# An attention and feed-forward layer in float32: the product with Wf in three F32R terms, and a new order of the steps around it

## What is computed

```python
Q = split_heads(x, 16); K = split_heads(x @ Wk + bk, 16); V = split_heads(x @ Wv + bv, 16)   # V: 1024 wide
o = softmax(Q @ K.T + causal_mask) @ V                       # per head, merged to 1024 features
x = layernorm(x + (x + gelu(o) @ Wf + bf))                   # exact gelu, Wf: 1024 x 256
h = silu(x @ wg.T / 127) * (x @ wu.T / 127)                  # 768 hidden features, integer weights
out = layernorm(x + h @ wd.T / 127)
```

## Time and profile before

| | us |
|---|---|
| runs (three) | 1847.09, 1849.84, 1851.43; median 1849.84 |
| the profiled execution | 1849.75 |
| its span (first to last instruction) | 1848.0 |
| TensorE busy | 1762.1 (95%) |
| VectorE busy | 1396.5 (76%) |
| GpSimd busy | 1221.8 (66%) |
| ScalarE busy | 1050.4 (57%) |

### The profile page before, as it was taken

How to read it: one execution, slowest core, us unless ns; L and a number is a source line. 1 busy time by engine, 2 the same in 40 slices (tenths; PEclk the granted TensorE clock), 3 DMA queues, 4 the chain that set the end, 5 groups by cost and what they waited for, 6 DMA issues and landing times. The chain is left out here.

```text
span 1848.0 us, 37611 instructions
## 1 busy us (share of the span) xinstructions
PE 1762.1 (95%) x10304; PEld 961.4 (52%) x10304; DVE 1396.5 (76%) x3417; ACT 1050.4 (57%) x1375; POOL 1221.8 (66%) x1146
## 2 busy tenths in 40 slices
PE   7999999999999999999999999888889999999996
PEld 5444444444444444444444444333466767676763
DVE  4787877778787787777778787886467878787864
ACT  2465665665565565665666565555545555555552
POOL 3488888888888888888888888999512222222221
PEclk9999999999999999999999999999999999999998
DMA  9675657556565655646556565563477565756500
GB/s 323 160 232 160 181 141 203 161 161 188 142 176 170 168 160 159 195 139 185 169 148 196 145 174 143 144 183 99 138 201 175 172 170 172 169 172 170 171 24 23
DMA packets 261152, 303.16 MB, mean 164 GB/s; under 512 B 28240, under 2 KB 177872, under 8 KB 261072
## 3 DMA queue, kind: packets, MB, share of 16 engines
q1 hardware_dynamic: 261072, 302.19, 58.3%
HBM read 174.20 MB, written 127.93 MB: 163 GB/s over the span
## 5 line engine op out<-in xcount | busy, mean ns | idle before, releaser
L802 POOL TENSOR_TENSOR weight_sum<-weight_sum,weights 128x512 f32<-128x512 f32 (+1 forms) x444 | 731.9, 1649 | 151.9 <-DVE weight_sum L1347 115.3
L1161 ACT ACTIVATE weights<-ring 128x1024 f32<-128x1024 f32 x576 | 570.7, 1026 | 221.2 <-PE ring L846 217.8
L846 PE MATMUL o_acc<-weights,v_pair 128*64 128x512 f32 (+3 forms) x3072 | 586.3, 501 | 17.1 <-POOL weights L757 16.4
L837 POOL TENSOR_TENSOR h_lo<-hidden,h_hi 128x512 f16<-128x512 f32 x96 | 114.4, 1193 | 390.2 <-ACT h_hi L1099 390.2
L1312 DVE TENSOR_REDUCE part_max<-ring 128x2 f32<-128x1024 f32 x256 | 301.0, 1217 | 86.4 <-PE ring L846 86.4
L846 PEld LDWEIGHTS o_acc<-weights,v_pair 128*64 128x64 f32 x3072 | 188.3, 136 | 302.7 <-issue 257.0
L1321 DVE CUSTOM_DVE_ANT_0 scrap<-ring,causal,part_max 128x256 bf16<-128x256 f32 (+3 forms) x512 | 251.3, 547 | 70.7 <-PE ring L846 70.4
L1321 DVE CUSTOM_DVE_ANT_0 scrap<-ring,causal 128x128 bf16<-128x128 f32 (+3 forms) x512 | 225.1, 486 | 91.1 <-PE ring L846 90.6
L846 PE MATMUL ring<-q_stack,k_stack 50*128 50x512 f32 (+3 forms) x1536 | 264.3, 382 | 26.1 <-DVE part_max L1312 17.6
L846 PE MATMUL ring<-k_stack,q_stack 48*128 48x512 f32 (+3 forms) x1536 | 256.9, 373 | 0.1
L846 PE MATMUL ring<-wf_sb,g 128*128 128x256 f32 x1024 | 230.5, 380 | 2.6 <-DVE y_pre L1416 1.7
(11 more groups left out here) (125 smaller groups left out, 2070.1 us busy)
## 6 DMA issues: line engine op xcount, KB each, us to landing
v_pairs<-v_unit SPq DMA_DIRECT2D x64, 512.0 KB, 3.5
v_pair<-v_pairs SPq DMA_DIRECT2D x64, 512.0 KB, 5.1
o_heads<-o_pair SPq DMA_DIRECT2D x64, 512.0 KB, 3.2
g<-o_heads SPq DMA_DIRECT2D x16, 2048.0 KB, 8.1
den_wide<-reciprocals SPq DMA_DIRECT2D x32, 1024.0 KB, 13.3
q_stack<-q_rows SPq DMA_DIRECT2D x128, 192.0 KB, 3.7
k_stack<-k_rows SPq DMA_DIRECT2D x128, 192.0 KB, 4.4
q_rows<-x_hi SPq DMA_DIRECT2D x28, 512.0 KB, 3.6
```

Of the source, the lines that this page charges most:

```text
L802: pool.tensor_tensor(dst, other, weights(t), ALU.add).then_inc(s_add, 1)
L837: pool.tensor_tensor(h_lo[:, f], h32[f % 2][:], h_hi[:, f], ALU.subtract).then_inc(s_hl, 1)
L846: return nc.tensor.matmul(o, l, r, start=start, stop=stop)
L1161: nc.scalar.activation(W[i][:], bank_of("t", i)[:], ACT.Exp).then_inc(s_w, 1)
```

## The change

Wf is split once into `wf_hi` and `wf_lo` (VectorE, in the drain of attention). Gelu's result is rounded by VectorE into `dn` (the buffer of the reciprocals, which are used by then) and the rest is made by GpSimd into `g`. TensorE multiplies with Wf as the stationary side and 512 tokens moving, 3 x 8 products for each half of the 256 features; the result has features on the partitions. x is loaded transposed, the residual sum `y_preT` is made in that layout, TensorE transposes it back, ScalarE copies it out. In the order: the products of unit r+1 now stand first on VectorE, ahead of z_pre; all Gelus are first on ScalarE; z of unit r-1 is made one step later; Wf's two halves stand around the transposes of y, and the transposes back between gate and up blocks 2 and 3; down goes over its six blocks for tiles 0 and 2 (two banks) and then 1 and 3. The stage has one step more (`STEPS_C = UNITS + 2`). The core of the diff:

```diff
 SyncE
 def load_g(r, it):                       # for unit r, issued two steps ahead
-    sp.wait_ge(s_wf, UT * (n - 1)); sp.wait_ge(s_y, UT * (n - 1))
+    sp.wait_ge(s_wf, DC * (n - 1)); sp.wait_ge(s_y, DC * (n - 1))
-    sp.dma_start(xn[r % 2][:], x[bass.ds(n * U, U), :].rearrange("(i p) d -> p i d", p=P))
+    sp.dma_start(xn[r % 2][:], xT[bass.ds(b, 1), :, t0:t0 + U].rearrange("o (c p) t -> (o p) c t", p=P))
 def load_dn(r, it):
-    sp.wait_ge(s_gn, HC * (n - 1))
+    sp.wait_ge(s_wf, DC * (n - 1))
 def finish(r, it):
-    if r >= 1: wait z of unit n - 1, store it
+    if r >= 2: wait z of unit n - 2, store it
 GpSimd
+def g_low(r, n, pairs):
+    for i in pairs:
+        pool.wait_ge(s_ghi, HC // 2 * n + i + 1)
+        pool.tensor_tensor(g[r % 2][:, 2*i:2*i+2], g_in[r % 2][:, 2*i:2*i+2],
+                           dn[r % 2][:, 2*i:2*i+2].bitcast(F32), ALU.subtract).then_inc(s_glo, 1)
 def attend(r, it):
+    if r == PAIRS + LEAD: g_low(0, 0, range(HC // 2))       # behind the last sums
 def finish(r, it):
+    if r + 1 < UNITS: g_low(r + 1, n + 1, range(0, HC // 2 - 1))
     ...                                                     # six h_lo of unit n - 1
+    if r + 1 < UNITS: g_low(r + 1, n + 1, range(HC // 2 - 1, HC // 2))
 TensorE
-def wf_product(r, n, tiles): ...
+def wf_product(r, n, d):
+    if d == 0 and r > 0: pe.wait_ge(s_yp, 2 * n)
+    for c in range(HC):
+        if d == 0 and c % 2 == 0: pe.wait_ge(s_ghi, HC // 2 * n + c // 2 + 1)
+        for k, w in enumerate((wf_hi, wf_lo)):
+            mm(rg[0][:, d], w[:, c, cols], dn[r % 2][:, c], c + k == 0, False)
+    for c in range(HC):
+        if d == 0 and c % 2 == 0: pe.wait_ge(s_glo, HC // 2 * n + c // 2 + 1)
+        e = mm(rg[0][:, d], wf_hi[:, c, cols], g[r % 2][:, c], False, c == HC - 1)
+    e.then_inc(s_wf, 1)
+def transpose_back(r, n):
+    pe.wait_ge(s_y, DC * (n + 1))
+    ...                                                     # 8 transposes of y_preT into ring0
 def attend(r, it):
-    if r == PAIRS + LEAD and b in (1, 3, 4): wf_product(0, 0, (max(b - 1, 1),))
+    if r == PAIRS + LEAD and b in (4, 5): wf_product(0, 0, b - 4)
 def down(m):
-    for i in range(UT):
-        for f in range(FC): ...
+    for tiles in ((0, 2), (1, 3)):
+        for f in range(FC): ...
 def finish(r, it):
-    wf_product(r, n, (0, 1)); transpose_y(r - 1, n - 1); wf_product(r, n, (2,))
-    gate_up(r - 1, n - 1); wf_product(r, n, (3,)); down(n - 1)
+    wf_product(r, n, 0); transpose_y(r - 1, n - 1); wf_product(r, n, 1)
+    gate_up(r - 1, n - 1, range(0, FC // 2)); transpose_back(r, n)
+    gate_up(r - 1, n - 1, range(FC // 2, FC)); down(n - 1)
 ScalarE
 def finish(r, it):
+    def copy_back():                                        # waits for s_yb; two copies of 128x512 into y_pre
+    if r + 1 < UNITS: gelus(r + 1, n + 1)
     ...                                                     # y_hi, Silu and h_hi as before
+    if f == 2 and r < UNITS: copy_back()
-    if r + 1 < UNITS: gelus(r + 1, n + 1)
     ...                                                     # logarithm and exponential
 VectorE
+def split_wf():
+    v.tensor_copy(wf_hi[:], wf_in[:])
+    v.tensor_tensor(wf_lo[:], wf_in[:], wf_hi[:].bitcast(F32), ALU.subtract)
+def g_high(r, n, pairs):
+    for i in pairs:
+        dve.wait_ge(s_gelu, HC * n + 2 * i + 2)
+        v.tensor_copy(dn[r % 2][:, 2*i:2*i+2], g_in[r % 2][:, 2*i:2*i+2]).then_inc(s_ghi, 1)
 def attend(r, it):
+    if r == PAIRS + LEAD and b == 0: g_high(0, 0, range(HC // 2))
+    if b == 0 and r == PAIRS + 1: split_wf()
 def finish(r, it):                                          # the new order
+    if r == 0: add_x()
+    norm(r + 1, it, range(HC // 2))
+    ...                                                     # waits for down, 4 x z_pre of unit n - 2
+    norm(r + 1, it, range(HC // 2, HC))
+    g_high(r + 1, n + 1, range(0, HC // 4))
+    ...                                                     # 2 x y_lo of unit n - 1
+    g_high(r + 1, n + 1, range(HC // 4, HC // 2))
+    if r > 0: add_x()       # 2 x (2 x + bf), tensor_scalar 128x512; 2 x y_preT = ring0 + xn
+    for f in range(FC):     # hidden f; after f = 0, 1 two z statistics; after f = 3, 4 two y statistics
+    ...                                                     # mean and variance, Newton, y of n, z of n - 2
```

## The result

The changed kernel takes 1956.88 us (median of four runs, 1955.76 to 1959.17) beside 1850.63 us of the kernel before (four runs on the same chip). The ratio is 1.058, 95% interval 1.056 to 1.059. The profiled execution took 1959.17 us, its span is 1957.4. The prediction was 1905 us with a range of 1842 to 1942: the direction was right, the loss is 106 us where 55 were forecast, and the time lies 15 us above the range.

A forecast was written before the change was run, and what follows sets the result against it. TensorE was taken to bound the kernel; the change would make a 33.8 us closed chain. Start +19, 13 steps x (33.8 - 30.6), end -4.5 gave +56 us on 1849.75: 1905 us, range 1842 to 1942.

The forecast's parts named there:

- The step: Second stage: one closed chain through VectorE, TensorE and ScalarE, 33.8 us instead of 30.6; 30.4 without either port wait.
- start and end: Step 2 starts 19 us later through Wf's splitting, first casts, remainders and loads; the last unit's end gains 4.5 us.
- Rival 3: TensorE's clock falls to half after idling before block 2; chain grows 2.7 us a step, 1940 us; chance 0.14.
- Newton's wait: VectorE's Newton steps held by GpSimd's fourth remainder: between 0 and 2.1 us, taken as 1.0.
- the chain to hidden 0: VectorE from first product through z_pre, roundings, doublings and residual sums to hidden 0: ends at 17.3 us.
- The two doublings: VectorE's two 128x512 doublings of x: 0.6 us each, scaled from the y rows, no wait for GpSimd's third remainder.
- rounding 3 behind the second remainder: VectorE's cast 3 against GpSimd's second g_low: wait between 0 and 2.4 us, taken as 2.4, ending at 14.2.
- wait before down: TensorE waits for h_lo before down, where the fourth Wf tile stood: some 1.7 us per step, new.
- ScalarE's copies and the statistics: Two copies back of 0.6 us each and the statistics: costed at nothing, standing between blocks while TensorE computes.
- the loads hidden: Reciprocals and g requested only after Wf: a loop of 30.5 us, hidden under the 33.8 us step.
- rivals 1 and 2: Rival 1: TensorE's saving reaches the end, 1842 us, chance 0.18. Rival 2: no difference, 1850 us, chance 0.08.
- TensorE's own loop: TensorE's work plus waits in the new order: 30.0 us a step, hardly under today's.

The follow-up runs named there:

- e3: Changed kernel with block 1 of gate and up computed three times, same result, to fill TensorE's idle time before block 2: 1925.46 us.
- e1: Changed kernel with no remainders made by GpSimd, the third term reading the rounded Gelu instead: 1873.49 us.
- e7: e2 with GpSimd's first three remainders after all four roundings, the fourth behind Newton's steps, and g requested without waiting for the residual sums: 1885.81 us.
- e4: Changed kernel with GpSimd's fourth remainder moved from behind the last h_lo to between the second and third h_lo: 1917.78 us.
- e9: e7 with down walking tile by tile instead of over two banks at once: 1894.10 us.
- e5: Changed kernel's new order with float32 Wf products of the Gelu itself, no splitting, roundings or remainders: 1893.96 us.
- e13: Changed kernel with freed loads, earlier doubling, z_pre first, remainders shared two each by GpSimd and VectorE, and a reordered first step: 1857.50 us.
- e2: Changed kernel with the doubling of x done one step earlier, behind hidden 2: 1881.86 us.

## Why the prediction was right in direction and half in size

The step was to be 33.8 us and is 37.57; start and end were to be 19 - 4.5 and are 23 - 4.6. Against the working, measured from the first product (1632.24):

| point in the step | forecast | measured | difference of the part |
|---|---|---|---|
| hidden 0 done | 17.3 | 17.66 (1649.90) | +0.4 |
| blocks 2 to 5 and transposes back done | 25.2 | 28.23 (1660.47) | +2.7 |
| h_hi 5 done | 27.3 | 30.6 (1662.85) | +0.3 |
| Newton's steps done, wait included | 31.0 | 34.9 (1667.16) | +0.6 |
| next first product | 33.8 | 37.55 (1669.79) | -0.2 |

**Failed: the clock.** This is the step that failed: half-speed work behind an idle time that the prediction's own schedule contained was left out of the sum. Rival 3 named the right place, condition and price: idle of 3.6 us before block 2 (3.74), half clock in blocks 2 and 3, 2.7 us a step (2.73 by e3). But it was held against the forecast as an alternative with a chance of 0.14, on the ground that the stretch was shorter than the one long stall of the earlier trace rows. The schedule that I had added up contained that stretch in every step; its consequence belonged in the sum. With it the step would have been 36.5 and the time 1940. The other 1.1 us is the second thing put too low: with Newton's wait whole as well, which the prediction gives as 34.9 without the clock, the same sum is 37.6 a step and 1955. Its range ended where only one of the two misfortunes is in, and both came, in every step. That 1955 lies so near 1956.88 is luck in part, by the next paragraph.

**Right by two errors: the chain to hidden 0.** It came out within 0.4 us, but not as added up. The two doublings were priced at 1.2 without a wait and take 2.96. The row I scaled, y, was the wrong one: four take 1.38, 0.33 apart with 256 elements, and the doublings in e1 are 0.40 apart with 512. Twice the width cost 0.07 more and not twice the time; whether that is a fixed part of each instruction or a difference between the two kinds is not shown. And they wait for GpSimd: they end 0.7 us behind its third remainder, a wait that the prediction names and puts at nothing. The Trainium skill, VectorE: DVE Perf Modes, section on the perf-mode tier table, gives an fp32 tensor_scalar in SBUF twice the rate of a tensor_tensor, and I followed the row; the measurement is nearer to the page (0.40 us from start to start against 0.60 for the products, a tensor_tensor of the same shape). On the other side a rounding takes 0.64 instead of 0.80, and GpSimd began its first remainder behind the first rounding, at 7.0, not behind the second, at 7.9; rounding 3 ended at 13.0 instead of 14.2.

**Half right: Newton's wait.** It was put between 0 and 2.1, at the middle, 1.0; it is 1.65, all that was left of the fourth remainder. By the Trainium skill, SBUF — State Buffer, section Who interferes with whom, it was to be the whole, and the rows agree: Newton's first step ends 0.03 us behind the remainder. Of y, which e7 shows to be held too, I had priced nothing. Where the remainder is put decides what it costs: between h_lo 2 and 3 (e4) it freed Newton's step, behind Newton's steps (e7) it met y.

**Right:** the F32R product (0.227 us: eight take 1.98 with the last one's tail); rounding 3 behind the second remainder, taken whole; 1.3 us of wait before down against 1.7; ScalarE's copies and the statistics at nothing; the loads hidden in a step of more than 31 us (30.5 was forecast for their loop, e1 shows 31.4); the end, -4.5 against -4.6; the start, 23 against 19. But of that start the 7 us at the end of attention vary: the last sum starts between 1316 and 1322 in the other kernels here, at 1316.30 in e9, which splits Wf, and at 1315.88 in e5, which does not. What the splitting and the first roundings cost there, forecast at 5, is therefore not shown, and the agreement may be luck.

**The prediction's rivals 1 and 2** asked for a chain that closes under 30.6. Even with no remainder made it closes at 31.4 by the loads, and only with these freed too at 29.98, which is the 30.0 that was forecast for TensorE's own loop.

## What to carry to other kernels

Where a schedule is added up and leaves TensorE idle for some microseconds in every turn, price the half-speed work behind it in the sum, not as a rival: here it was 2.7 of 7 us, and laying useless products into the gap won 31 us. Work given to GpSimd to relieve VectorE can come back on VectorE's chain: beside a remainder of 2.3 us, roundings, doublings, Newton's steps and y were held until it ended, while hidden blocks, residual sums and statistics were not (e7). So choose what it runs beside, and look at what stands behind it on GpSimd. Shared out over both engines (e13) the four remainders cost 0.7 us a step against none at all, where they had cost 6. And before a saving on the busiest engine is counted, look at how short the other loops are: 2 us a step less on TensorE were worth 5 us in all with the loads freed and no remainders made, and the kernel lost 106 with those loops as they were.

## What was not expected of the hardware

- The same idle time of 3.1 us before block 2 was followed by 0.43 us between products in one step and by 0.22 in another (e4); with 3.7 to 3.8 us it was half clock in every step (the changed kernel), with 0.85 to 0.94 in none (e2). And in e9 the clock fell to 0.50 for 3.4 us behind three short waits of 0.16, 1.33 and 0.72 us, in some steps and not in others.
- y, a subtraction and product with two pointer operands, 128x256, is held by a GpSimd remainder (3.43 instead of 1.38 us for four, e7), as are an addition and product of 128x8 (Newton, 1.82 instead of 0.17) and roundings.
- Where a VectorE rounding and a GpSimd remainder were both ready, they took turns, each for a whole instruction: three remainders, 6.98 us in one piece (e7), took 8.18 with roundings before and between them.
